# A recommender top on one core: one-hot products moved a period ahead, and a reordered head

## The chip, the cores and the metric

The kernel runs on one core of a Trainium2 chip. The metric is the device time of one execution in microseconds (us), as the median of several runs; lower is better.

## What is computed

The reference looks up 26 embedding rows for each of 2048 samples, forms all pairwise products of the 27 feature vectors of a sample (26 rows and a dense vector, 128 numbers each), and sends the result through three layers:

```python
e = jnp.stack([tbl_0[ids[:, 0]], ..., tbl_25[ids[:, 25]]], axis=1)     # (2048, 26, 128)
combined = jnp.concatenate([dense_output[:, None, :], e], axis=1)      # (2048, 27, 128)
interactions = jnp.einsum('bfd,bgd->bfg', combined, combined)
z = jnp.concatenate([dense_output, interactions[:, iu, ju]], axis=1)   # upper triangle, 351 pairs
h = jnp.concatenate([z, r_dense_output], axis=1)
h = jnp.maximum(h @ W_top1 + b_top1, 0.0)                              # 607 -> 512
h = jnp.maximum(h @ W_top2 + b_top2, 0.0)                              # 512 -> 256
y = h @ W_top3                                                         # 256 -> 1
```

All is float32. Eight of the tables have 1000 rows; the others have 1000 to 125000.

## The kernel before

**Tiling.** A duo is 256 samples (8 duos), a super is two duos (4 supers). A group is a pair of gathered tables for one duo: 18 tables are gathered, so a duo has 9 groups (T_GROUPS), 72 in all. The other 8 tables, of 1000 rows each, lie in SBUF as 125 partitions of 8 rows, each split in a rounded part (tab_hi) and a remainder (tab_lo), and are looked up by products with one-hot matrices.

**The steps**, as the code names them:
- "T": a group. POOL has gathered it in four indirect DMAs (line 239) into one of 5 slots of E; PE turns it (line 307, four transposes) into a PSUM bank; ACT copies it into ET (line 486).
- "hot": a chunk of one-hot products. DVE builds the one-hot of a chunk (line 552, ring of 3, so three chunks ahead of PE), PE multiplies (line 322, 8 matmuls: 4 blocks of rows, tab_hi and tab_lo). A duo has 16 chunks. Four chunks fill one bank, which ACT empties into ET (line 501). DVE needs the indices of four chunks from one transfer into oidx, a ring of 3 (line 247).
- "gram": 8 products of four samples' features with themselves (line 347) into one of two psG buffers; ACT copies one quarter (line 508), DVE places three more (line 574). A duo has 8 such fills. They read the ET half of their duo; ET has two halves, by d % 2.
- "C", "K": per super, the gram columns are turned (line 358) and copied to U (line 433), then turned as pairs (line 372), rounded (ACT, line 512) and split (DVE, line 583).
- "part": parts 0 to 3 are the first layer (lines 386 and 391, emptied at 460 and 462), 4 and 5 the second (line 398), 6 the third (line 405).

**What sets the order.** `steps_of(d)` writes out by hand the steps of period d, and PE, ACT, DVE and SP each go through the same list and do their share of each step, in order. Period d holds the turns of duo d, the grams of duo d - 1, chunks 8 to 15 of duo d between the grams, and chunks 0 to 7 of duo d + 1 after them; period 0 holds the first 24 chunks (all of duo 0, half of duo 1). Even periods add columns, pairs and parts 0 and 1 of a super, odd ones its parts 2 to 6. Period 8, the tail, has the last duo's grams and the last super's layers. `place_fills` gives the fills of T, hot, C, K and part one of three banks each, in step order. POOL only goes through the groups: it waits for the turn of group n - 5 before it gathers group n.

**The head.** SP issues the first part of the gather indices, then index transfers, the tables, the second part of the gather indices, the dense inputs, then the weights, and after these, going through the steps, the further index transfers from the fourth on (chunks 12 to 15 of duo 0), each once the one-hot that frees its place in the ring is built. The raw tables come into ET's second half, in six places (RAW), so tables 6 and 7 wait for the split of tables 0 and 1. ACT first makes tab_hi of all eight tables (`round_table`, line 469), then starts on the steps. DVE builds three one-hots, splits two tables (line 557), and then splits one more at every second chunk of period 0.

Of the kernel before, what the change touches and what calls it, by code (L numbers as in the profile page):

```python
# [13 lines left out]
def dlrm_program(nc, dense_pairs, dense_rows, gather_idx, hot_idx, gathered, small, W1_dense, W1_pairs,  # L14
# [20 lines left out]
    ROWS_P = ROWS // ROWS_K  # L35
    CHUNK_K = 4
    CHUNKS = NS * ROWS_K // CHUNK_K
    HALF_CHUNKS = CHUNKS // 2
    FILL_CHUNKS = 2 * ROWS_K // CHUNK_K
    RING = 3  # L40
    ID_RING = 3
    RAW = 6
    BANKS = 3

# [4 lines left out]
    KP = 3  # L49
# [9 lines left out]

    def steps_of(d):  # L60
        turns = [("T", d * T_GROUPS + i) for i in range(T_GROUPS)] if d < DUOS else []
        late = [("hot", d, c) for c in range(HALF_CHUNKS, CHUNKS)] if d < DUOS else []
        early = [("hot", d + 1, c) for c in range(HALF_CHUNKS)] if d + 1 < DUOS else []
        grams = [("gram", d - 1, i) for i in range(G_FILLS)]
        if d == 0:
            hot = [("hot", 0, c) for c in range(CHUNKS)] + early
            steps = hot[:4]
            for i, turn in enumerate(turns):
                steps += [turn] + hot[4 + 2 * i:6 + 2 * i]
            return steps + hot[4 + 2 * T_GROUPS:]  # L70
        if d == TAIL:
            u = SUPERS - 1
            return (grams + [("C", u, b) for b in range(C_BANKS)] + [("K", u, k) for k in range(KP)] +
                    [("part", u, p) for p in range(PARTS)])
        steps = []
        for i in range(G_FILLS):
            steps += [grams[i], late[i]]
            if i % 2 == 1:
                steps.append(turns[i // 2])
        rest = turns[G_FILLS // 2:]  # L80
        if d >= 2 and d % 2 == 0:
            u = d // 2 - 1
            columns = [("C", u, b) for b in range(C_BANKS)]
            pairs = [("K", u, k) for k in range(KP)]
            for i in range(HALF_CHUNKS):
                steps += early[i:i + 1] + columns[i:i + 1]
                if i % 2 == 1:
                    steps.append(rest[i // 2])
            steps += [pairs[0], pairs[1], rest[4], pairs[2]]
            return steps + [("part", u, 0), ("part", u, 1)]  # L90
        parts = [("part", d // 2 - 1, p) for p in range(2, PARTS)] if d >= 3 else []
        for i in range(HALF_CHUNKS):
            steps += early[i:i + 1]
            if i % 2 == 1:
                steps += [rest[i // 2]] + parts[i // 2:i // 2 + 1]
        return steps + [rest[4]] + parts[4:]

    PERIODS = range(TAIL + 1)
    STEPS = [step for d in PERIODS for step in steps_of(d)]
# [30 lines left out]
    with ctx:  # L130
# [114 lines left out]
        def _(sp):  # L245
# [5 lines left out]
                sp.dma_start(dense[:, d % 2], dense_pairs[d]).then_inc(dense_in[d % 2], 16)  # L251

            def load_table(h):
                sp.dma_start(raw_table(h), small[h].rearrange("(p k) d -> p (k d)", k=ROWS_K)  # L254
                             ).then_inc(table_in[h], 16)

            first = T_GROUPS * 4
            sp.dma_start(gidx[:, 0:first], gather_idx[:, 0:first]).then_inc(gidx_in[0], 16)
            load_oidx(0)
            load_table(0)  # L260
            load_table(1)
            sp.dma_start(gidx[:, first:], gather_idx[:, first:]).then_inc(gidx_in[1], 16)
            for h in range(2, RAW):
                load_table(h)
                if h == 3:
                    load_oidx(1)
                    load_oidx(2)
            load_dense(0)
            load_dense(1)
            for h in range(RAW, NS):  # L270
                sp.wait_ge(lo_ready, h - RAW + 1)
                load_table(h)
            sp.dma_start(raw_w1d, W1_dense.rearrange("a p n -> p a n")).then_inc(w1d_in, 16)
            sp.dma_start(raw_w1p, W1_pairs.rearrange("(k p) n -> p k n", k=KP)).then_inc(w1p_in, 16)
            sp.dma_start(w2[:, :, :], W2.rearrange("(k p) n -> p k n", p=P)).then_inc(weights_in, 16)
# [189 lines left out]
        @block.scalar  # L465
        def _(act):
            def round_table(h):
                act.wait_ge(table_in[h], 16)
                nc.scalar.copy(tab_hi[0:ROWS_P, h].rearrange("p k d -> p (k d)"),  # L469
                               raw_table(h)).then_inc(hi_ready, 1)  # L470

# [41 lines left out]

            act.wait_ge(ident_ready, 1)
            nc.scalar.copy(ident_r[:, :], ident[:, :]).then_inc(ident_r_ready, 1)
            for h in range(NS):
                round_table(h)
            for d in PERIODS:
                if d == 1:
                    round_W1()  # L520
# [4 lines left out]
                for step in steps_of(d):  # L525
                    if step[0] == "T":
                        empty_gathered(step[1])
                    elif step[0] == "hot" and step[2] % FILL_CHUNKS == FILL_CHUNKS - 1:
                        empty_hot(step[1], step[2])
                    elif step[0] == "gram":  # L530
                        empty_gram_first(step[1], step[2])
                    elif step[0] == "C" and on_scalar(step[1], step[2]):
                        empty_columns(nc.scalar, step[1], step[2])
                    elif step[0] == "K":
                        round_pairs(step[1], step[2])
                    elif step[0] == "part" and step[2] % 2 == 0:
                        empty_part(nc.scalar, step[1], step[2])
# [144 lines left out]
```

## Time and profile before

| | us |
|---|---|
| median of 3 runs (431.76 to 432.88) | 431.84 |
| the profiled execution | 434.48 |
| its span, first to last instruction | 432.7 |
| PE busy (matmuls) | 369.9 (86%) |
| POOL busy | 276.1 (64%) |
| DVE busy | 256.5 (59%) |
| ACT busy | 114.2 (26%) |
| mean granted TensorE clock | 0.942 |

The profile was taken of one execution, which was 2.6 us over the median; 1.8 us of it lie outside the span. Issuing of DMAs isn't counted as busy, so POOL's share is only the part of a gather that its engine records. Matmuls overlap, and a busy PE isn't PE at its peak. A clock of 1.00 is 2.4 GHz, one of 0.50 is 1.2 GHz.

### The profile page before, as it was taken

The numbers are of one execution on the slowest core, as the hardware profiler recorded it, in microseconds if no ns is written. First come the engines' busy times: TensorE is split into PE (matmuls) and PEld (weight loads), VectorE is DVE, ScalarE is ACT, GpSimd is POOL, SyncE is SP. The second block draws the span as 40 slices with busy tenths as digits, with TensorE's granted clock in tenths as the row PEclk, the third lists the DMA queues.
The fourth block names the chain that finished last, engine by engine and source line by source line (L and its number), as shares of the span: only waits on it lengthen the run. The fifth ranks groups of instructions, "written<-read, shape, count | busy, mean of one in ns | idle before, by whom it ended". The sixth has DMA issues, their size and how long they took to land.

```text
span 432.7 us, 6765 instructions
## 1 busy us (share of the span) xinstructions
PE 369.9 (86%) x2792; PEld 332.1 (77%) x2792; DVE 256.5 (59%) x368; ACT 114.2 (26%) x235; POOL 276.1 (64%) x295
## 2 busy tenths in 40 slices
PE   0560499996499959999999999999999999999797
PEld 0450499996499948997799979986999799678663
DVE  3254199998088833875389838952588566106410
ACT  2110333322122331322232333322123412321210
POOL 6772277777777777777777777777777777710000
PEclk9996599999599969999999999999899999989999
DMA  5659535444244433444343424343433332310000
GB/s 129 178 165 231 183 84 117 87 79 101 52 93 79 98 56 54 87 100 106 55 91 79 103 52 92 78 100 79 93 77 77 56 53 53 78 21 0 2 0 1
DMA packets 50941, 35.89 MB, mean 83 GB/s; under 512 B 6136, under 2 KB 44664, under 8 KB 50912
## 3 DMA queue, kind: packets, MB, share of 16 engines
q0 software_dynamic: 41472, 18.89, 24.7%
q1 hardware_dynamic: 9440, 16.58, 13.0%
q8 instruction: 22, 0.36, 0.3%
q14 instruction: 7, 0.06, 0.0%
HBM read 35.44 MB, written 0.01 MB: 82 GB/s over the span
## 4 chain that ended last, share of the span: by engine, by line
PE 58%; POOL 18%; issue 7%; DMA 6%; SPq 5%; DVE 3%; ACT 2%; DVEq 0%
POOL E L239 18%; PE psG L347 17%; PE psB L322 16%; PE psB L391 8%; PE psB L398 6%; DMA ET<-tbl 6%; PE psB L386 4%; PE psB L307 3%; SPq L254 2%; PE psB L358 2%; PE psB L405 2%; SPq L251 1%; SPq L247 1%; DVE S L574 1%; PE psB L372 1%
## 5 line engine op out<-in xcount | busy, mean ns | idle before, releaser
L239 POOL DMA_INDIRECT E<-tbl,gidx x288 | 275.4, 956 | 103.9 <-issue 87.0
L552 DVE TENSOR_TENSOR one_hot<-oidx,psR 125x1024 fp32r<-125x1024 int32 x128 | 152.3, 1215 | 39.0 <-PE psB L322 32.2
L322 PE MATMUL psB<-one_hot,tab_hi 125*128 125x256 f32 x512 | 143.2, 311 | 19.5 <-DVE tab_lo L557 13.4
L322 PE MATMUL psB<-one_hot,tab_lo 125*128 125x256 f32 x512 | 133.4, 292 | 0.0
L322 PEld LDWEIGHTS psB<-one_hot,tab_hi 125*128 125x128 f32 x512 | 103.0, 201 | 21.7 <-issue 13.8
L347 PE MATMUL psG<-ET 128*108 128x108 f32 x1024 | 112.5, 265 | 2.0 <-ACT ET L486 1.0
L347 PEld LDWEIGHTS psG<-ET 128*108 128x108 f32 x1024 | 106.6, 180 | 3.1 <-DVE S L574 1.6
L574 DVE COPY_PREDICATED S<-own,psG 108x216 f32<-108x216 int32 x192 | 77.1, 402 | 51.1 <-ACT S L508 44.5
L322 PEld LDWEIGHTS psB<-one_hot,tab_lo 125*128 125x128 f32 x512 | 103.1, 201 | 0.6 <-issue 0.5
L307 PE MATMUL psB<-ident_r,E 128*128 128x128 f32 x288 | 36.7, 253 | 32.0 <-ACT ET L501 18.3
L307 PEld LDWEIGHTS psB<-ident_r,E 128*128 128x128 f32 x288 | 31.0, 145 | 36.4 <-issue 20.0
L486 ACT COPY ET<-psB 128x512 f32<-128x512 f32 x72 | 42.3, 589 | 62.1 <-PE psB L307 62.0
L508 ACT COPY S<-psG 108x216 f32<-108x216 f32 x64 | 21.7, 340 | 110.1 <-PE psG L347 109.3
L398 PE MATMUL psB<-UH,w 128*128 128x512 f32 x64 | 29.0, 599 | 0.0
L462 DVE TENSOR_SCALAR UH<-psB,b1s 128x512 f32<-128x512 f32 x8 | 6.0, 751 | 36.6 <-PE psB L391 36.6
L501 ACT COPY ET<-psB 128x512 f32<-128x512 f32 x32 | 18.8, 586 | 30.9 <-PE psB L322 30.9
L391 PE MATMUL psB<-Zp_hi,w1p_hi 128*128 128x512 f32 x48 | 26.2, 545 | 0.0
L398 PEld LDWEIGHTS psB<-UH,w 128*128 128x128 f32 x64 | 11.7, 189 | 12.1 <-issue 12.0
L391 PE MATMUL psB<-Zp_hi,w1p_lo 128*128 128x512 f32 x48 | 19.3, 402 | 0.0
L391 PE MATMUL psB<-Zp_lo,w1p_hi 128*128 128x512 f32 x48 | 19.3, 401 | 0.0
L469 ACT CAST tab_hi<-ET 125x1024 fp32r<-125x1024 f32 x8 | 8.4, 1045 | 38.4 <-DMA ET<-tbl 38.4
L386 PE MATMUL psB<-Zd,w1d 128*128 128x512 f32 x32 | 18.0, 645 | 0.6 <-DVE Zp_lo L583 0.5
(34 smaller groups left out, 149.7 us busy)
## 6 DMA issues: line engine op xcount, KB each, us to landing
oidx<-hot_idx SPq DMA_DIRECT2D x32, 256.0 KB, 3.5
E<-tbl,gidx POOLq DMA_INDIRECT x288
ET<-tbl SPq DMA_DIRECT2D x8, 500.0 KB
dense<-dense_pairs SPq DMA_DIRECT2D x8, 128.0 KB, 3.6
Zd<-dense_rows SPq DMA_DIRECT2D x4, 256.0 KB, 3.1
UH<-W_pairs SPq DMA_DIRECT2D x1, 768.0 KB, 18.6
S<-W_dense SPq DMA_DIRECT2D x1, 512.0 KB, 21.1
w<-W SPq DMA_DIRECT2D x1, 512.0 KB, 13.4
```

Source lines behind the costliest of these rows:

```text
L239: nc.gpsimd.indirect_dma_start(E[:, n % SLOTS, i, :], None, gathered[2 * (n % T_GROUPS) + i // 2].bitcast(f32r), bass.IndirectOffsetOnAxis ...
L307: turned = nc.tensor.transpose(bank[:, i * P:(i + 1) * P].bitcast(f32r), E[:, n % SLOTS, i, :], ident_r[:, :])
L322: product = nc.tensor.matmul(bank[:, t % 2 * DUO:(t % 2 + 1) * DUO], tab[0:ROWS_P, t, r, :], one_hot[0:ROWS_P, m % RING, kc, :], start=(r ...
L347: gram = nc.tensor.matmul(psG[g % 2][0:M, a // 4, a % 4 * M:(a % 4 + 1) * M], four, four, start=True, stop=True)
L386: nc.tensor.matmul(bank[:, :], w1d[:, cols], Zd[:, :], start=True, stop=False)
L391: layer = nc.tensor.matmul(bank[:, :], w[:, kp, cols], z[:, kp, :], start=False, stop=(kp == KP - 1 and w is w1p_lo))
L398: layer = nc.tensor.matmul(bank[:, :], w2[:, q, cols], h1[:, q, :], start=(q == 0), stop=(q == M1 - 1))
L486: nc.scalar.copy(features(d, 1 + 2 * pair, 2), bank[:, :].rearrange("p (f j s) -> p f j s", f=2, s=GROUP)).then_inc(emptied, 1)
L501: nc.scalar.copy(features(d, f, 2), psB[bank][:, :].rearrange("p (f j s) -> p f j s", f=2, s=GROUP)).then_inc(bank_out[bank], 1)
L508: nc.scalar.copy(gram_rows(d, i), gram_samples(g, 0)).then_inc(G_first[g % 2], 1)
L552: nc.vector.tensor_tensor(one_hot[0:ROWS_P, m % RING], ids, rows, ALU.is_equal).then_inc(hot_full[m % RING], 1)
L574: copied = nc.vector.copy_predicated(gram_rows(d, i), mine, gram_samples(g, q))
```

## The change

- Chunks: `steps_of` puts all 16 chunks of duo d + 1 in period d, behind the 8 gram fills of duo d - 1. Period 0 has all 32 chunks of duos 0 and 1 (five, then three behind each turn), period 7 none.
- Between the grams stand the turns 0 to 3 of the duo and, in odd periods, parts 2 and 3; between the chunks stand turns 4 to 8, and columns and pairs or parts 4 to 6. Parts 0 and 1 stay at the end of even periods. In period 7 the last turn comes behind part 6.
- ACT rounds two tables before the steps and the other six at chunks 0, 2, 4, 6, 8 and 10 of duo 0.
- Each table comes in two transfers, of 112 and of 13 partitions, and ACT waits for both.
- SP: the second index transfer and the first dense load come behind three tables; the third index transfer behind six; the second part of the gather indices and the second dense load behind all tables.

```diff
+    SPREAD_P = ROWS_P // 16 * 16
...
-        late = [("hot", d, c) for c in range(HALF_CHUNKS, CHUNKS)] if d < DUOS else []
-        early = [("hot", d + 1, c) for c in range(HALF_CHUNKS)] if d + 1 < DUOS else []
+        hots = [("hot", d + 1, c) for c in range(CHUNKS)] if d + 1 < DUOS else []
         grams = [("gram", d - 1, i) for i in range(G_FILLS)]
         if d == 0:
-            hot = [("hot", 0, c) for c in range(CHUNKS)] + early
-            steps = hot[:4]
+            hots = [("hot", 0, c) for c in range(CHUNKS)] + hots
+            steps = hots[:5]
             for i, turn in enumerate(turns):
-                steps += [turn] + hot[4 + 2 * i:6 + 2 * i]
-            return steps + hot[4 + 2 * T_GROUPS:]
+                steps += [turn] + hots[5 + 3 * i:8 + 3 * i]
+            return steps
...
+        among_grams = {i: [turns[i // 2]] for i in range(1, G_FILLS, 2)}
+        rest = turns[G_FILLS // 2:]
+        among_hots = {1 + 3 * i: [turn] for i, turn in enumerate(rest)}
+        if d % 2 == 0:
+            u = d // 2 - 1
+            for b in range(C_BANKS):
+                among_hots.setdefault(3 + b, []).append(("C", u, b))
+            for k in range(KP):
+                among_hots.setdefault(12 + k, []).append(("K", u, k))
+            late = [("part", u, 0), ("part", u, 1)]
+        else:
+            u, late = d // 2 - 1, []
+            if u >= 0:
+                for i, p in enumerate(range(2, M1)):
+                    among_grams.setdefault(2 + 3 * i, []).append(("part", u, p))
+                for i, p in enumerate(range(M1, PARTS)):
+                    among_hots.setdefault(3 + 4 * i, []).append(("part", u, p))
         steps = []
         for i in range(G_FILLS):
...
+            steps += [grams[i]] + among_grams.get(i, [])
+        for i in range(CHUNKS):
+            steps += hots[i:i + 1] + among_hots.get(i, [])
+        return steps + late
...
             def load_table(h):
-                sp.dma_start(raw_table(h), small[h].rearrange("(p k) d -> p (k d)", k=ROWS_K)
-                             ).then_inc(table_in[h], 16)
+                rows = small[h].rearrange("(p k) d -> p (k d)", k=ROWS_K)
+                for part in (slice(0, SPREAD_P), slice(SPREAD_P, ROWS_P)):
+                    sp.dma_start(raw_table(h)[part], rows[part]).then_inc(table_in[h], 16)
...
             load_oidx(0)
-            load_table(0)
-            load_table(1)
-            sp.dma_start(gidx[:, first:], gather_idx[:, first:]).then_inc(gidx_in[1], 16)
-            for h in range(2, RAW):
+            for h in range(RAW):
                 load_table(h)
-                if h == 3:
+                if h == 2:
                     load_oidx(1)
-                    load_oidx(2)
-            load_dense(0)
-            load_dense(1)
+                    load_dense(0)
+            load_oidx(2)
             for h in range(RAW, NS):
                 sp.wait_ge(lo_ready, h - RAW + 1)
                 load_table(h)
+            sp.dma_start(gidx[:, first:], gather_idx[:, first:]).then_inc(gidx_in[1], 16)
+            load_dense(1)
...
-                act.wait_ge(table_in[h], 16)
+                act.wait_ge(table_in[h], 32)
...
-            for h in range(NS):
+            for h in range(2):
                 round_table(h)
+            rounded_tables = 2
...
-                    elif step[0] == "hot" and step[2] % FILL_CHUNKS == FILL_CHUNKS - 1:
-                        empty_hot(step[1], step[2])
+                    elif step[0] == "hot":
+                        if d == 0 and step[2] % 2 == 0 and rounded_tables < NS:
+                            round_table(rounded_tables)
+                            rounded_tables += 1
+                        if step[2] % FILL_CHUNKS == FILL_CHUNKS - 1:
+                            empty_hot(step[1], step[2])
```

## Rows read from the trace of the kernel before

Timeline rows: start us, us, engine, line, operation, out<-in with shapes, count, and in brackets the engine's idle time before and what ended it.

**Rows 1.** Waits, whole span: who waited for whom, total us, times, longest us

```profile
POOL E L239 <- issue: 87.0, 285, 0.3
POOL E L239 <- PE psB L307: 14.9, 1, 14.9
```

**Rows 2.** Timeline of POOL: the first gather, three others, the last

```profile
3.27 1.09 POOL L239 DMA_INDIRECT E<-tbl,gidx  x1 [1.70 <-DMA gidx<-gather_idx]
...
30.55 0.94 POOL L239 DMA_INDIRECT E<-tbl,gidx  x1 [0.31 <-issue]
...
50.69 0.94 POOL L239 DMA_INDIRECT E<-tbl,gidx  x1 [14.93 <-PE psB L307]
...
111.28 0.94 POOL L239 DMA_INDIRECT E<-tbl,gidx  x1 [0.31 <-issue]
...
379.92 0.94 POOL L239 DMA_INDIRECT E<-tbl,gidx  x1 [0.30 <-issue]
```

**Rows 3.** Timeline of PE: turns that end a duo, and the tail's grams

```profile
113.78 0.75 PE L307 MATMUL psB<-ident_r,E 128*128 128x128 f32 x4 [4.40 <-DMA E<-tbl,gidx]
115.50 0.85 PE L347 MATMUL psG<-ET 128*108 128x108 f32 x3 [0.98 <-ACT ET L486]
...
382.61 0.82 PE L307 MATMUL psB<-ident_r,E 128*128 128x128 f32 x4
...
385.86 6.41 PE L347 MATMUL psG<-ET 128*108 128x108 f32 x48
...
392.46 3.29 PE L347 MATMUL psG<-ET 128*108 128x108 f32 x32 [0.20 <-DVE S L574]
```

**Rows 4.** Windows: length, busy PE PEld DVE ACT POOL, PEclk, DMA share, GB/s

```profile
32.00:50.00 18.00, 0.31 (x3) 0.34 (x3) 4.71 (x4) 4.51 (x7) 3.15 (x3) 0.57 0.78 212
...
109.70:120.00 10.30, 5.24 (x27) 5.09 (x28) 0.79 (x2) 1.22 (x3) 7.55 (x10) 0.50 0.29 51
...
154.00:164.00 10.00, 7.04 (x25) 5.12 (x25) 2.08 (x3) 2.93 (x5) 7.56 (x9) 0.50 0.31 55
...
168.00:214.00 46.00, 45.36 (x347) 39.65 (x346) 30.10 (x43) 11.63 (x24) 34.71 (x38) 1.00 0.40 85
214.00:256.80 42.80, 42.09 (x354) 39.46 (x354) 31.11 (x46) 14.02 (x32) 32.12 (x36) 1.00 0.39 81
...
347.30:385.90 38.60, 37.92 (x284) 31.91 (x282) 17.43 (x32) 10.34 (x22) 25.34 (x27) 1.00 0.30 55
385.90:432.70 46.80, 40.28 (x243) 31.51 (x243) 15.00 (x33) 8.01 (x21) 0.00 (x0) 0.94 0.00 1
```

**Rows 5.** Timeline of ACT: first and last table cast, and the first emptying

```profile
9.61 1.04 ACT L469 CAST tab_hi<-ET 125x1024 fp32r<-125x1024 f32 x1 [7.28 <-DMA ET<-tbl]
...
48.02 1.04 ACT L469 CAST tab_hi<-ET 125x1024 fp32r<-125x1024 f32 x1 [2.84 <-DMA ET<-tbl]
48.97 0.58 ACT L501 COPY ET<-psB 128x512 f32<-128x512 f32 x1
```

**Rows 6.** DMA issues, 0 to 60 us: count, KB each, median us to landing

```profile
oidx<-hot_idx SPq DMA_DIRECT2D x6, 256.0 KB, 6.8
...
dense<-dense_pairs SPq DMA_DIRECT2D x2, 128.0 KB, 18.8
```

**Rows 7.** Timeline of SP's queue: two of its longest rows

```profile
33.22 7.24 SPq L275 DMA_DIRECT2D w<-W  x1
...
47.31 10.52 SPq L247 DMA_DIRECT2D oidx<-hot_idx  x3
```

**Rows 8.** Timeline of DVE: one-hots built without a wait

```profile
59.66 15.91 DVE L552 TENSOR_TENSOR one_hot<-oidx,psR 125x1024 fp32r<-125x1024 int32 x14
```

**Rows 9.** Chain that ended last, in order: start us, us, what

```profile
168.14 1.52 PE psG L347 x16
169.65 0.97 PE psB L322 x8
...
173.42 1.57 PE psG L347 x16
```

More of the change, by code:

```diff
@@ L37, in dlrm_program @@
     CHUNKS = NS * ROWS_K // CHUNK_K
-    HALF_CHUNKS = CHUNKS // 2
     FILL_CHUNKS = 2 * ROWS_K // CHUNK_K
@@ L74, in steps_of @@
                     [("part", u, p) for p in range(PARTS)])
+        among_grams = {i: [turns[i // 2]] for i in range(1, G_FILLS, 2)}
[15 more added lines that the diff above has]
+                    among_hots.setdefault(3 + 4 * i, []).append(("part", u, p))
         steps = []
         for i in range(G_FILLS):
[L77 to L96, printed above, removed]
+            steps += [grams[i]] + among_grams.get(i, [])
+        for i in range(CHUNKS):
+            steps += hots[i:i + 1] + among_hots.get(i, [])
+        return steps + late
     PERIODS = range(TAIL + 1)
```

## The prediction

> **What bounds the kernel now.** I first asked for the waits of the whole span [rows 1]. POOL, which issues the 288 gathers of line 239, is held up by another engine exactly once, for 14.9 us; its other gaps are 0.3 us of its own issue. The POOL timeline [rows 2] shows the place: the 24th gather ends at 35.76 us (50.69 less 14.93), the next starts at 50.69. Outside that hole one gather takes 0.94 + 0.30 = 1.24 us, so a duo's 36 gathers take 44.8 us, and the last one (379.92 + 0.94) ends at 380.86. Nothing else delays POOL, so the last gather can only come earlier if the hole closes or the long gathers at the head shorten.
>
> Is the last gather what the end waits for? The turn of the last group starts at 382.61 [rows 3], 1.75 us after that gather; the turn of the 18th group, for which PE did wait (4.40 us, on the gather), started 1.56 us after its gather (111.28 + 0.94 = 112.22). So PE arrives at the last turn within about 0.2 us of its data: both queues end together. After it come part 6 of the perceptron (3.25 us from the turn's start to the first gram), then 46.8 us of tail with POOL empty [rows 4].
>
> The windows [rows 4] give PE's load by period: 46.0 us for period 3 (odd: five perceptron parts), 42.8 for period 4 (even: columns, pairs, two parts), 38.6 for period 7. The mean of an odd and an even one, 44.4, is 0.4 under POOL's 44.8. A head change that speeds up POOL alone would therefore gain almost nothing, because PE would be late next; that is why the second half of the change matters.
>
> Why the hole: ACT rounds all 8 tables before it empties any bank. The casts start between 9.61 and 48.02 us, 5.5 us apart on average, and the first emptying is at 48.97 [rows 5]. PE has three banks, fills them, and stops; POOL has five slots, fills them and one more, and stops.
>
> **The change, step by step.**
>
> 1. ACT rounds two tables ahead, the other six at every second one-hot chunk. Same eight casts, no new work. The turns then need banks emptied early, which ACT now does. Gain up to 14.9 us on POOL. New waiting order: behind each cast stand the emptyings, so a late table still holds the banks.
>
> 2. Tables in 112 + 13 partitions. Before, one table of 500 KB lands each 5.5 us (93 GB/s), though in 32 to 50 us the queues together moved 212 GB/s at a share of 0.78 [rows 4, 5]. Dense loads of 128 KB took 18.8 us to land [rows 6]: behind the tables something is far fuller than the mean share says. The price is 8 more issues on SP. An issue that isn't blocked takes 0.3 to 0.6 us; the two rows at [rows 7] that last 7 and 10 us are blocked or waiting ones. Eight at 0.5 are 4 us of SP, beside transfers that take longer.
> The Trainium skill (DMA: Bandwidth & Descriptors, "Why a DMA increments its semaphore by 16 and not by 1") says that such a copy is spread over the largest number up to 16 that divides its outer size: 5 engines for 125 rows, 16 for 112, 13 for 13. The slow landing of the tables at a middling share agrees. By the rule the tables would cease to be the limit; the sum doesn't use it beyond the bounds in step 3.
>
> 3. Period 0 now holds 32 chunks instead of 24, and three chunks instead of two between turns. So the turn of group 3 needs the one-hot of chunk 13, and that needs the fourth index transfer (chunks 12 to 15). This transfer stands on SP behind everything of the head: the tables, the second part of gidx, both dense loads, W1, W2, biases, Zd. That is the new dependency. Before, it was issued at 47.31 and with 6.8 us landed at 54.1 [rows 6, 7]; nobody minded, as the turns had come to a halt for other reasons. Bytes up to and including it: tables 4000, four index transfers 1024, W1 1280, W2 512, Zd 256, dense 256, gidx 144 KB, in all 7.65 MB. Gathers take 65.6 KB per 1.24 us = 53 GB/s beside it. At 212 GB/s in all, 159 are left: 48 us, landing at 49.5. At 212 / 0.78 = 272, 219 are left: 35 us, landing at 36.5. I take 36, since 272 is what the engines gave while they were busy and that is what an even spread should reach.
> After the landing DVE owes three operations of 1.14 us (chunk 12, the eighth split, chunk 13; pace from 14 builds in 15.91 us [rows 8]), then PE one chunk, at most 1.94 us (twice the 0.97 of [rows 9]), and a turn: some 6 us, so the turn of group 3 is done at 42. When is it needed? Group 5's gathers start at 30.55 [rows 2], group 8's three groups of 4.98 later, at 45.5, and they need the slot of group 3. So 3.5 us to spare: no stall. Later turns follow three chunks apart, 3.4 us by DVE's pace when PE is at 2.4 GHz, against POOL's 4.98.
> **Sum of steps 1 to 3: -14.9 us on POOL** (at worst, from landing at 49.5: a new hole of 49.5 + 6 - 45.5 = 10 us).
>
> 4. All one-hot products one period early. The work is the same (128 chunks of 0.97 us, 64 gram fills of 1.52 [rows 9]); eight chunks, 7.8 us, move from period 7 to period 0. Period 0 then ends at about 61 us, bound by DVE: after the landing at 36 it has some 22 operations of 1.14 left. Period 1 is 8 fills, 16 chunks at DVE's 1.14 and 9 turns of 0.30 (168.14 to 173.42, less two fills and two chunks [rows 9]), 33 us, so 94. POOL's last group for it, without the hole, lands at 98.9 (the turn that waited for it started at 113.78 [rows 3], less 14.9). So PE has caught up with POOL by the end of period 1, with eight chunks more done than before. From there an even period must end 9.3 us after POOL's last group (two chunks, pair 2, parts 0 and 1 come after the last turn), an odd one somewhat later, and the sum of both is 88.8 against 89.6: PE stays level. In period 7 PE needs 38.6 - 7.8 = 30.8; it starts 9.3 behind, so it is ready for the last turn after about 40 of POOL's 44.8 us. **Four to five us of slack, on the path nothing.** The gain of the move is that step 1's 14.9 us aren't swallowed by PE.
>
> 5. Grams without chunks between them. In the tail, where they already run so, two fills take 3.29 us and a wait of 0.20 for DVE's placing [rows 3]. In a period two fills and a turn are 2 x 1.52 + 0.30 = 3.34. Loss 0.15 x 4 = 0.6 us a period; in odd periods parts 2 and 3 lie between and cover it. I take +0.5 in all, after slack; if it were 0.6 in each of periods 3 to 7 and clock losses came on top, it reaches +4.
>
> 6. End of period 7: part 6 now comes before the last turn. From the last turn's start to the first gram it was 3.25 us; where nothing stood between, at period 2's start, it was 1.72 (113.78 to 115.50) [rows 3]. **-1.5 us.**
>
> 7. Clock. PE now waits about 3 us before the last turn. After such waits the granted clock was 0.50 for 10.3 us (109.7 to 120 [rows 4]), that is 1.2 GHz. In the tail of before only the first gram fills were slow: three in the first 6.6 us, where the warm pace gives 3.49 for two. A longer slow stretch costs 0 to 2.5 more; **+1.5.**
>
> Total: -14.9 + 0 + 0.5 - 1.5 + 1.5 = -14.4 us. Profiled: span 432.7 to 418.3, its time 434.48 to 420.1. The median of the runs, 431.84, is 2.6 below the profiled execution; the same sum makes it **417.4**.
>
> **Rivals.**
> A. The head's fourth index transfer is late. For it: SP is in order, and 7.65 MB stand before it. Against it: the transfers of before were slow at a low mean share. Landing at 49.5 makes a hole of 10 us: 427. If the split brought nothing at all and it landed at 54.1 as before, 14.6 us: 432, no change. This is also the case that the change doesn't do what it says.
> B. PE becomes the bound in periods 3 to 7: its slack of 4 to 5 us is eaten by one clock stretch (10.3 us at half pace costs up to 5.1) and by the gram blocks (3): 4 us past the slack, 421.
> C. Slower: the clock. With eight chunks out of the way PE waits for gathers in each of periods 2 to 7, where in the trace it waits for none after period 2. Place: those waits; price: 5.1 us for a stretch like that of 109.7; it decides from the fourth stretch on (4 x 5.1 less the slack of 4.5 is 15.9, more than the gain of 14.4). With six, 30.6 - 4.5 = 26 us: 443.5. Against it: a slow PE falls behind, then doesn't wait, and recovers; before shows two stretches (109.7 and 154 [rows 4]) and none of that length later.
> The Trainium skill (TensorE: Matmul & The Clock Gate, "HAM oscillation — how this bites in real kernels") tells of kernels in which each wait for data throttles the engine anew, which speaks against this change; by it C would be the outcome. The trace has the effect twice, and shows it ending when PE falls behind.
>
> **Chances.** Forecast (415 to 420) 0.62; A with a partial hole (420 to 430) 0.12; B (419 to 424) 0.17; A in full, about 432, 0.04; C 0.05. Range: step by step the low end is 414 (no clock loss, slightly shorter issue of the head's gathers: the six groups before the hole end at 35.76, where 3.27 + 24 x 1.24 would be 33.0), the high end 425, which leaves out C, the full A and half of the partial one. About 1.3 us, 0.3%, can be told from no change: faster 0.91, same 0.04, slower 0.05.
>
> **What would show it.** The POOL timeline without a gap over 0.4 us: steps 1 to 3 right; a gap at the group after 45 us, with DVE waiting for oidx before it: A. Tables landing 2 to 3 us apart: step 2. PE waiting 2 to 5 us for the last gather in period 7: step 4; no wait there and parts back to back: B. The first gram 1.7 us after the last turn's start: step 6. Granted clock under 0.9 in periods 3 to 7: C. The prediction is wrong if the last gather ends elsewhere than at 366, or if the stretch from it to the end isn't 52 us.

## The result, and the profile after

| | before | changed |
|---|---|---|
| median, us | 432.36 (431.76 to 433.13, 4 runs) | 420.91 (419.24 to 422.60, 4 runs) |
| profiled execution, us | 434.48 | 419.24 |
| its span, us | 432.7 | 417.0 |
| mean granted clock | 0.942 | 0.965 |

The ratio is 0.9734, with a 95% interval of 0.9691 to 0.9778. The kernel is faster by 11.4 us in the medians and by 15.7 us in the two profiled spans: the profiled execution of the kernel before lies above all four of its runs, that of the changed kernel is the fastest of its four. What follows explains the 15.7 us of the two traces, some 4 us more than the medians differ by. The forecast was 417.4, in a range of 414 to 425. Medians are of all executions of a kernel in its job; where too few of them lay within 1.5% of its fastest, no ratio is given.

The POOL timeline of the changed kernel (start us, us, engine, line, operation; in brackets the idle time before) stands against [rows 2]. Line 239 is now line 240.

```profile
28.47 1.85 POOL L240 DMA_INDIRECT E<-tbl,gidx  x1 [0.30 <-issue]
...
39.34 1.89 POOL L240 DMA_INDIRECT E<-tbl,gidx  x1 [0.31 <-issue]
...
47.75 0.94 POOL L240 DMA_INDIRECT E<-tbl,gidx  x1 [0.30 <-issue]
...
365.86 0.94 POOL L240 DMA_INDIRECT E<-tbl,gidx  x1 [0.31 <-issue]
```

The hole is gone. The last gather ends at 366.80 instead of 380.86: 14.1 us, against a hole of 14.9. The missing 0.8 to 0.9 us are small things: the gathers are busy 275.9 us instead of 275.4 (two of 1.85 and 1.89 us in the head are shown), and their gaps without the hole are 89.3 instead of 89.0, with a start of the first gather that is 0.07 later.

ACT's timeline, against [rows 5]: the casts of the tables, now 1.2 to 4.8 us apart (2.9 on average) instead of 5.5, with emptyings between them.

```profile
8.20 1.04 ACT L469 CAST tab_hi<-ET 125x1024 fp32r<-125x1024 f32 x1 [5.87 <-DMA ET<-tbl]
10.38 1.04 ACT L469 CAST tab_hi<-ET 125x1024 fp32r<-125x1024 f32 x1 [1.14 <-DMA ET<-tbl]
12.88 1.04 ACT L469 CAST tab_hi<-ET 125x1024 fp32r<-125x1024 f32 x1 [1.46 <-DMA ET<-tbl]
...
20.62 0.58 ACT L486 COPY ET<-psB 128x512 f32<-128x512 f32 x1
...
28.32 1.05 ACT L469 CAST tab_hi<-ET 125x1024 fp32r<-125x1024 f32 x1 [0.17 <-DMA ET<-tbl]
```

DVE's timeline shows the new dependency of step 3, the fourth index transfer:

```profile
29.43 1.21 DVE L557 TENSOR_TENSOR one_hot<-oidx,psR 125x1024 fp32r<-125x1024 int32 x1
38.05 1.22 DVE L557 TENSOR_TENSOR one_hot<-oidx,psR 125x1024 fp32r<-125x1024 int32 x1 [7.42 <-DMA oidx<-hot_idx]
39.19 1.22 DVE L562 TENSOR_TENSOR tab_lo<-ET,tab_hi 125x1024 fp32r<-125x1024 f32 x1
```

Last, PE at the end of period 7, against [rows 3]: the last turns (line 307), parts 5 and 6 (lines 398 and 405), the first gram of the tail.

```profile
358.40 0.53 PE L307 MATMUL psB<-ident_r,E 128*128 128x128 f32 x4 [1.75 <-DMA E<-tbl,gidx]
358.77 3.67 PE L398 MATMUL psB<-UH,w 128*128 128x512 f32 x8
363.44 0.53 PE L307 MATMUL psB<-ident_r,E 128*128 128x128 f32 x4 [1.01 <-DMA E<-tbl,gidx]
363.81 1.91 PE L405 MATMUL psB<-w3s,h 128*128 128x1 f32 x16
368.41 0.75 PE L307 MATMUL psB<-ident_r,E 128*128 128x128 f32 x4 [2.69 <-DMA E<-tbl,gidx]
369.99 4.19 PE L347 MATMUL psG<-ET 128*108 128x108 f32 x23 [0.83 <-issue]
```

So the 15.7 us of the spans come as follows: last gather 14.1 earlier; its turn 1.6 us behind it instead of 1.75 (0.1); first gram 1.58 us after the turn's start instead of 3.25 (1.7); tail 47.0 us instead of 46.8 (-0.2).

### The profile page after: what moved, and what is told of

The parts are those of the page before. It is cut to its first block, busy times and chain, and to the rows that moved or that the text cites. A ratio compares the mean times of both kernels' runs of the same rounds, so it can differ in the third digit from the quotient of the medians.

```text
span 417.0 us, 6773 instructions
## 1 busy us (share of the span) xinstructions
PE 365.8 (88%) x2792; PEld 328.6 (79%) x2792; DVE 257.2 (62%) x368; ACT 114.4 (27%) x235; POOL 276.7 (66%) x295
## 3 DMA queue, kind: packets, MB, share of 16 engines
q1 hardware_dynamic: 9632, 16.58, 14.9%
## 4 chain that ended last, share of the span: by engine, by line
POOL 53%; PE 23%; issue 18%; DMA 3%; DVE 2%; ACT 1%; POOLq 0%
POOL E L240 53%; PE psG L347 7%; PE psB L391 5%; PE psB L322 4%; DMA E<-tbl,gidx 2%; PE psB L386 2%; PE psB L398 2%; PE psB L358 2%; PE psB L307 1%; DVE S L579 1%; PE psB L372 1%; DVE one_hot L557 1%; PE psB L405 0%; DMA gidx<-gather_idx 0%; DVE Zp_lo L588 0%
## 5 line engine op out<-in xcount | busy, mean ns | idle before, releaser
L240 POOL DMA_INDIRECT E<-tbl,gidx x288 | 275.9, 958 | 89.3 <-issue 87.0
L557 DVE TENSOR_TENSOR one_hot<-oidx,psR 125x1024 fp32r<-125x1024 int32 x128 | 149.3, 1214 | 35.5 <-PE psB L322 23.4
L322 PE MATMUL psB<-one_hot,tab_hi 125*128 125x256 f32 x512 | 139.1, 307 | 21.4 <-DVE tab_lo L562 11.1
L322 PE MATMUL psB<-one_hot,tab_lo 125*128 125x256 f32 x512 | 131.0, 290 | 0.0
L347 PE MATMUL psG<-ET 128*108 128x108 f32 x1024 | 108.8, 265 | 3.5 <-DVE S L579 2.3
L347 PEld LDWEIGHTS psG<-ET 128*108 128x108 f32 x1024 | 104.7, 180 | 6.1 <-DVE S L579 3.3
L307 PEld LDWEIGHTS psB<-ident_r,E 128*128 128x128 f32 x288 | 29.9, 143 | 24.3 <-DMA E<-tbl,gidx 23.6
L391 PE MATMUL psB<-Zp_hi,w1p_hi 128*128 128x512 f32 x48 | 25.2, 526 | 0.0
L358 PE MATMUL psB<-ident,S 108*128 108x108 f32 x104 | 16.3, 287 | 1.8 <-issue 1.8
L386 PE MATMUL psB<-Zd,w1d 128*128 128x512 f32 x32 | 16.7, 603 | 0.5 <-DVE Zp_lo L588 0.5
```

Of the source, the lines that this page charges most:

```text
L240: nc.gpsimd.indirect_dma_start(E[:, n % SLOTS, i, :], None, gathered[2 * (n % T_GROUPS) + i // 2].bitcast(f32r), bass.IndirectOffsetOnAxis ...
L307: turned = nc.tensor.transpose(bank[:, i * P:(i + 1) * P].bitcast(f32r), E[:, n % SLOTS, i, :], ident_r[:, :])
L322: product = nc.tensor.matmul(bank[:, t % 2 * DUO:(t % 2 + 1) * DUO], tab[0:ROWS_P, t, r, :], one_hot[0:ROWS_P, m % RING, kc, :], start=(r ...
L347: gram = nc.tensor.matmul(psG[g % 2][0:M, a // 4, a % 4 * M:(a % 4 + 1) * M], four, four, start=True, stop=True)
L358: turned = nc.tensor.transpose(bank[:, i * M:(i + 1) * M], S[0:M, :, c], ident[0:M, 0:M])
L386: nc.tensor.matmul(bank[:, :], w1d[:, cols], Zd[:, :], start=True, stop=False)
```

## The experiments

**Which part of the change closes the hole?** Four kernels, run on one chip together with the kernel before (434.28, 431.74 to 438.04, 19 runs). The kernel before took 1.9 us longer here than in the job of the result (432.36), and the changed kernel wasn't in this job; the expectations were worked out from the figures of that one.

*head_only*: the new head with the old steps (an extract, against the changed kernel).

```diff
     def steps_of(d):
...
+        late = [("hot", d, c) for c in range(HALF_CHUNKS, CHUNKS)] if d < DUOS else []
+        early = [("hot", d + 1, c) for c in range(HALF_CHUNKS)] if d + 1 < DUOS else []
```

> The head of the changed kernel (split table transfers, SP's order, ACT rounding between chunks) with the steps of the kernel before. Theory 1, the prediction's step 4: PE, level with POOL before, is late next and swallows the 14.9 us; last gather near 366 but last turn 8 to 14 us behind its data, 428 to 431 us. Theory 2: PE stood still in the same hole, so both queues move together; last turn within 1 us of its data, part 6 still behind it, 418 to 420 us.

Measured: 421.79 us (419.05 to 423.42), ratio 0.9666 (0.9586 to 0.9746). The time is 1.8 us above theory 2's 418 to 420, in a job in which the kernel before took 1.9 us longer, and well under theory 1's 428 to 431: theory 1 falls. PE at the end of its period 7:

```profile
366.89 0.86 PE L307 MATMUL psB<-ident_r,E 128*128 128x128 f32 x4
...
370.69 0.86 PE L307 MATMUL psB<-ident_r,E 128*128 128x128 f32 x4
372.19 1.92 PE L405 MATMUL psB<-w3s,h 128*128 128x1 f32 x16 [0.64 <-ACT ET L486]
373.97 6.40 PE L347 MATMUL psG<-ET 128*108 128x108 f32 x48
```

Its last gather ends at 366.14 (the group's turn waits for it no longer), so with the 1.6 us of the changed kernel its data are there at 367.7 and the turn comes 3 us late, not within 1 us as theory 2 had it, and not 8 to 14. With part 6 behind it the first gram is at 373.97, 4.0 us later than in the changed kernel's trace: 2.3 because the turn is later (370.69 against 368.41), 1.7 for part 6's place (3.28 us from turn to gram against 1.58), which is step 6 and not the chunks. The best executions of both kernels are level (419.05 and 419.24), and the intervals overlap. So the move of the chunks is worth between nothing and the 2.3 us of these two traces, not the whole gain.

*move_only*: the new steps with the old head, each table in one transfer again (an extract).

```diff
             def load_table(h):
-                rows = small[h].rearrange("(p k) d -> p (k d)", k=ROWS_K)
-                for part in (slice(0, SPREAD_P), slice(SPREAD_P, ROWS_P)):
-                    sp.dma_start(raw_table(h)[part], rows[part]).then_inc(table_in[h], 16)
+                sp.dma_start(raw_table(h), small[h].rearrange("(p k) d -> p (k d)", k=ROWS_K)
+                             ).then_inc(table_in[h], 16)
...
             first = T_GROUPS * 4
             sp.dma_start(gidx[:, 0:first], gather_idx[:, 0:first]).then_inc(gidx_in[0], 16)
             load_oidx(0)
+            load_table(0)
+            load_table(1)
...
-            for h in range(2):
+            for h in range(NS):
                 round_table(h)
```

> The steps of the changed kernel with the head of the kernel before. Theory 1 (POOL is the bound, its hole stays near 14.9 us): last gather at 381 as before, gain only from the last turn's order, 429.5 to 432 us. Theory 2 (PE was the bound from period 3 on): the 7.8 us taken out of period 7 show, 423 to 426 us.

Measured: 432.92 us (432.49 to 435.74, 10 runs), ratio 0.9953 (0.9917 to 0.9989). Theory 1 in the mechanism: 0.9 us above its 429.5 to 432, and far from theory 2's 423 to 426. POOL's hole is where it was:

```profile
34.73 0.94 POOL L240 DMA_INDIRECT E<-tbl,gidx  x1 [0.31 <-issue]
50.67 0.94 POOL L240 DMA_INDIRECT E<-tbl,gidx  x1 [15.00 <-PE psB L308]
```

The 0.5% that is left, some 2 us, is of the size of step 6 (the last turn's order). PE at the end of this trace:

```profile
382.20 0.53 PE L308 MATMUL psB<-ident_r,E 128*128 128x128 f32 x4 [1.50 <-DMA E<-tbl,gidx]
383.56 7.61 PE L348 MATMUL psG<-ET 128*108 128x108 f32 x48 [0.83 <-issue]
```

The first gram is 2.3 us earlier than before (383.56 against 385.86), 1.9 of it between turn and gram (1.36 against 3.25). But this execution's tail took 50.3 us instead of 46.8; that comes up again under step 7.

*act_first*: the changed kernel, ACT rounding all tables first.

```diff
-            for h in range(2):
+            for h in range(NS):
                 round_table(h)
-            rounded_tables = 2
+            rounded_tables = NS
```

> The changed kernel, but ACT rounds all eight tables before it empties a bank, as before. Theory 1 (the split alone closes the hole): last table lands near 27.6, ACT is free near 29, turn of group 1 before the 35.5 at which POOL needs its slot; no hole, within 1 us of the changed kernel, 420 to 422 us. Theory 2 (ACT's order closes it): a hole of 8 us or more, 428 us or more.

Measured: 421.42 us (419.08 to 422.58), ratio 0.9657 (0.9586 to 0.9729). Theory 1: the interleaving on ACT is worth nothing once the tables come fast, and POOL waits for PE nowhere in this trace. ACT's last cast and first emptyings:

```profile
26.96 1.05 ACT L469 CAST tab_hi<-ET 125x1024 fp32r<-125x1024 f32 x1 [1.25 <-DMA ET<-tbl]
27.91 0.58 ACT L501 COPY ET<-psB 128x512 f32<-128x512 f32 x1
28.39 0.41 ACT L492 COPY ET<-dense 128x256 f32<-128x256 f32 x1
28.69 0.59 ACT L486 COPY ET<-psB 128x512 f32<-128x512 f32 x1
```

The first emptying is at 27.91 instead of 48.97; the kernel before ran out of slots at 35.76.

*no_spread*: the changed kernel, each table in one transfer.

```diff
-                rows = small[h].rearrange("(p k) d -> p (k d)", k=ROWS_K)
-                for part in (slice(0, SPREAD_P), slice(SPREAD_P, ROWS_P)):
-                    sp.dma_start(raw_table(h)[part], rows[part]).then_inc(table_in[h], 16)
+                sp.dma_start(raw_table(h), small[h].rearrange("(p k) d -> p (k d)", k=ROWS_K)
+                             ).then_inc(table_in[h], 16)
```

> The changed kernel, but each table in one transfer of 125 partitions. Theory 1, rival A of the prediction: the fourth index transfer lands near 54 behind slow tables, the turn of group 3 ends near 60, POOL has a hole of 12 to 15 us in the ninth group, 430 to 434 us. Theory 2 (ACT's interleaving alone suffices): no hole, 420 to 423 us.

Measured: 434.93 us (433.91 to 436.19, 10 runs), ratio 1.0014 (0.9978 to 1.0050): the whole gain is gone. Theory 1 (0.9 us above its 430 to 434), rival A of the prediction. Its POOL and DVE timelines, where three holes have come in place of one:

```profile
36.55 0.94 POOL L240 DMA_INDIRECT E<-tbl,gidx  x1 [1.95 <-PE psB L306]
...
44.73 0.94 POOL L240 DMA_INDIRECT E<-tbl,gidx  x1 [3.52 <-PE psB L306]
...
62.42 0.94 POOL L240 DMA_INDIRECT E<-tbl,gidx  x1 [13.03 <-PE psB L306]
```

```profile
44.71 1.21 DVE L556 TENSOR_TENSOR one_hot<-oidx,psR 125x1024 fp32r<-125x1024 int32 x1
56.52 1.22 DVE L556 TENSOR_TENSOR one_hot<-oidx,psR 125x1024 fp32r<-125x1024 int32 x1 [10.59 <-DMA oidx<-hot_idx]
```

DVE gets the indices at 56.5, PE's turn of group 3 starts at 61.69, and POOL, which needs that slot, goes on at 62.42. The long hole is the ninth group's, as rival A has it.

So of the head's parts the split of the transfers carries the gain: without it all is lost, without ACT's new order nothing is. SP's new order wasn't tried by itself, and neither was the kernel before with nothing but the split.

**What binds now?** The remaining kernels ran in later hours, when the kernel before itself took 527 to 530 us; their times can be compared with it and with each other in the same job, not with those above, and the changed kernel wasn't in these jobs. None of their expectations, which are in us of the usual hours, can be judged by the times; what they still tell stands in the traces.

*part6_last*: part 6 behind the last turn of period 7, as before.

```diff
+        if d == DUOS - 1:
+            steps.remove(("part", u, PARTS - 1))
+            late = [("part", u, PARTS - 1)]
         return steps + late
```

> The changed kernel with part 6 behind the last turn of period 7, as before. Theory 1 (step 6 of the prediction): from the last turn's start to the first gram 3.2 to 3.3 us instead of 1.6, so 1.6 us slower than the changed kernel, about 422.5 us. Theory 2: PE's longer idle time ahead of the last turn cools the clock as well, 423 to 425 us.

Measured: 515.58 us (501.63 to 520.1) beside 527.3 for the kernel before. In this trace the last two turns stand together:

```profile
466.69 1.53 PE L310 MATMUL psB<-ident_r,E 128*128 128x128 f32 x8
468.19 1.92 PE L408 MATMUL psB<-w3s,h 128*128 128x1 f32 x16
469.97 5.26 PE L350 MATMUL psG<-ET 128*108 128x108 f32 x36
```

The last four of the eight transposes start at 467.68, 1.6 us behind the last gather (466.08), so the first gram comes 2.3 us after the last turn's start: 0.7 more than the changed kernel's 1.6, and less than the 3.25 of before, where PE also waited 0.65 us for ACT ahead of part 6. Inconclusive by itself; the usual hours tell more: 3.25 us (before) and 3.28 (head_only) with part 6 behind the turn, 1.36 (move_only) and 1.58 (the changed kernel, act_first, no_spread) without.

*chunks_back*: chunks 8 to 15 of the last duo back between the grams of period 7.

```diff
+        if d == DUOS - 2:
+            hots = hots[:CHUNKS // 2]
+        back = [("hot", d, c) for c in range(CHUNKS // 2, CHUNKS)] if d == DUOS - 1 else []
         for i in range(G_FILLS):
-            steps += [grams[i]] + among_grams.get(i, [])
+            steps += [grams[i]] + back[i:i + 1] + among_grams.get(i, [])
```

> The changed kernel, but chunks 8 to 15 of the last duo go back into period 7, between its grams. Theory 1 (step 4's slack): PE waited 1.75 + 1.01 + 2.69 = 5.5 us for gathers in period 7; 7.8 us more work make the last turn 2.3 us later, and PE has no idle time that cools the clock; 421 to 424 us. Theory 2 (the slack has no worth): same as the changed kernel within 1 us, the clock giving back what the work takes. Theory 3 (the move carries the gain): 427 us or more.

Measured: 516.14 us (512.95 to 517.98), ratio to the kernel before of that job 0.9774 (0.9694 to 0.9854). It keeps a gain of the relative size of the changed kernel's (0.9734). Theory 3's 427 us would be 0.988 of 432.36, or 0.983 of 434.28, which the interval includes, and a gain in per cent need not carry over to these hours. So it speaks against theory 3 only weakly; head_only is the evidence against it. Theories 1 and 2 aren't told apart.

*fewer_gathers* and its repeats: the fourth gather of each group of duos 3 and 4 is left out, so the outputs lack the rows that it would have brought.

```diff
-                for i in range(4):
+                for i in range(3 if n in FEWER else 4):
                     nc.gpsimd.indirect_dma_start(
```

> The changed kernel without the fourth gather of each group of duos 3 and 4 (18 gathers, 22.4 us of POOL, left out; the turn takes what lies in the slot). Theory 1 (POOL alone is the bound): 22 us faster, 399 us. Theory 2 (PE is level with POOL from period 2 on, with the 5.5 us of waits in period 7 and a few in periods 4 and 6 as all its slack): 5 to 9 us faster, 412 to 416 us, and PE waits for no gather in period 7.

> The changed kernel without the fourth gather of each group of duos 3 and 4 (18 gathers, 22.4 us of POOL left out, the turn takes what lies in the slot), on another chip. Theory 1 (POOL alone is the bound): 22 us faster, 399 us. Theory 2 (PE is level with POOL; its 5.5 us of waits in period 7 and some in periods 4 and 6 are all its slack): 5 to 9 us faster, 412 to 416 us, no wait of PE for a gather in period 7.

> The changed kernel without the fourth gather of each group of duos 3 and 4 (18 gathers, 22.4 us of POOL left out, the turn takes what lies in the slot), taken again in the same hour. Theory 1 (POOL alone is the bound): 22 us faster, 399 us. Theory 2 (PE is level with POOL; its 5.5 us of waits in period 7 and some in periods 4 and 6 are all its slack): 5 to 9 us faster, 412 to 416 us, no wait of PE for a gather in period 7.

Measured: 498.78, 494.95 and 495.02 us beside 527.3, 530.12 and 526.55; ratios 0.9473 (0.9403 to 0.9542) in the first and 0.9381 (0.9304 to 0.9458) in the third. Beside chunks_back in the first job it is 17.4 us faster. The turns of these traces show where: from the last turn of duo 2 to that of duo 4 it is 118.0 us in chunks_back (190.10 to 308.09) and 97.7 in fewer_gathers (184.32 to 282.06). In all traces of these hours it is 113.6 to 119.7 with all gathers (five traces) and 97.0 to 98.4 without (three). The other duos scatter: duo 5 takes 60.1 in both of the first job, duo 6 48.3 in chunks_back and 56.7 in fewer_gathers. So 15 to 23 us are saved just where gathers are missing, of their 22.4, although POOL waited for PE for 58 to 70 us in these traces (0.6 us in the changed kernel's trace), 38 us of it around these two duos (190 to 310 us of fewer_gathers). The first theory's size comes out under conditions in which it should not, and the second's test, the slack in a usual hour, wasn't had. Inconclusive for the question it was made for.

*half_first* and its repeats: the last duo is gathered in another order, all 18 tables of its first 128 samples and then those of the second, so that four of its gram fills can run in period 7 in PE's waits.

```diff
+        if d == DUOS - 1:
+            for i, turn in enumerate(turns[5:]):
+                at = steps.index(turn) + 1 + (i == 2)
+                steps.insert(at - (i == 2), ("gram", d, i))
...
+    def source(n, i):
+        if n // T_GROUPS < DUOS - 1:
+            return i % 2, 2 * (n % T_GROUPS) + i // 2
+        return divmod(4 * (n % T_GROUPS) + i, NG)
```

> The changed kernel, with the last duo gathered in another order: all 18 tables of its first 128 samples, then those of the second; its first four gram fills then run in period 7, in the gaps where PE waits for gathers. Theory 1: the tail loses four fills of 1.75 us, period 7 gains at most 1 us, and PE stays warm into the tail; 6 to 8 us faster than the changed kernel, 413 to 415 us. Theory 2: PE's 5.5 us of waits don't hold four fills of 1.52 us and their evictions, the last turn comes late by 3 us or more: 416 to 419 us.

> The changed kernel with the last duo gathered half by half of its samples, and four of its gram fills in period 7, as in half_first, on another chip. Theory 1: four fills of 1.75 us leave the tail, 6 to 8 us faster than the changed kernel's 420.9, 413 to 415 us. Theory 2: the four fills don't fit in PE's waits of period 7, the last turn comes 3 us or more late: 416 to 419 us.

> The changed kernel with the last duo gathered half by half of its samples, and four of its gram fills in period 7, taken again in an hour in which the kernel before should run near its usual 432 to 434 us. Theory 1: four fills of 1.75 us leave the tail; 6 to 8 us faster than the changed kernel's 420.9, so 413 to 415 us. Theory 2: the four fills don't fit in PE's waits of period 7, the last turn comes 3 us or more late: 416 to 419 us.

Measured: 513.67, 504.36 and 510.89 us beside 527.3, 530.12 and 526.55; ratios 0.9528 (0.9468 to 0.9587) in the second and 0.9739 (0.9674 to 0.9804) in the third. PE around the last turn (line 318; grams are line 361) in the third:

```profile
450.55 1.73 PE L361 MATMUL psG<-ET 128*108 128x108 f32 x16
452.06 0.52 PE L318 MATMUL psB<-ident_r,E 128*128 128x128 f32 x4
452.41 1.73 PE L361 MATMUL psG<-ET 128*108 128x108 f32 x16
...
457.73 1.73 PE L361 MATMUL psG<-ET 128*108 128x108 f32 x16
...
461.02 0.51 PE L318 MATMUL psB<-ident_r,E 128*128 128x128 f32 x4
461.37 3.25 PE L361 MATMUL psG<-ET 128*108 128x108 f32 x32
```

From the last turn's start to the end of the span it is 40.6 us here (501.6 - 461.02), 40.5 in the first run and 42.9 in the second, against 48.6 in the changed kernel (417.0 - 368.41) and 48.3 to 50.4 in chunks_back and the three fewer_gathers, in the hours of these runs: the stretch behind the last turn is 5.4 to 9.9 us shorter, as theory 1 has it. But the last turn starts 7.3, 11.1 and 7.3 us behind the last gather in the three runs, where it is 1.6 to 6.3 in the other traces of these hours, so theory 2's late turn may be in it too. Whether the end comes earlier when PE isn't late anyway, and so whether this kernel beats the changed one, stays open: it was never timed against it under the usual conditions.

## Why the prediction was right

The time is in the range and the mechanism of the head is the one that was forecast, but the number needed some luck. 420.91 lies just above the 415 to 420 that was called the forecast and given 0.62, and inside B's and A's brackets, though neither happened: POOL has no hole, and PE waited for the last gather. One step, the fourth, was wrong in its conclusion. By terms of the two traces:

| us | forecast | traces |
|---|---|---|
| steps 1 to 3, last gather | -14.9 | -14.1 |
| step 4, last turn behind its gather | 0 | -0.1 |
| step 5, gram blocks | +0.5 | 0 |
| step 6, turn to first gram | -1.5 | -1.7 |
| step 7, tail | +1.5 | +0.2 |
| sum | -14.4 | -15.7 |

By its own signs the prediction was to be wrong if the last gather ended elsewhere than at 366 or the stretch from it to the end wasn't 52 us. They are 366.80 and 50.2: the first is 0.8 off, the second 2, for steps 5 and 7, and the two errors partly cancel.

- **Steps 1 to 3, the hole.** Forecast 14.9 us, no new hole; measured 14.1, no new hole. The load of the head was the point that decided. The fourth index transfer was put at 36; DVE got it at 38.05. Group 3's turn was put at 42, ended at 44.1 (start 43.47), and POOL needed it at 47.75. The rate that was taken, 272 GB/s from the busy share of 32 to 50 us, was about right: the changed kernel moved 251 over its first 36 us. Most of the transfer's parts were there in time for the 36.5 (11 of 16 by 36.13), the last at 38.03. The other bound, 212, would have made a hole, and no_spread, where the head's transfers stay slow, has it: 13.0 us, and a kernel no faster than before. Rival A was priced at 432 for that case; 434.9 was measured. It was right that the split decides; it was wrong that ACT's order has a share (step 1's "up to 14.9"): act_first shows none.
- **Step 2, the split.** Over 4 to 24 us the changed kernel moved 253 GB/s, the one with single transfers 173.

```profile
4.00:24.00 20.00, 10.19 (x61) 9.31 (x61) 15.24 (x14) 7.55 (x9) 15.42 (x16) 1.00 1.14 253
```

```profile
4.00:24.00 20.00, 6.78 (x28) 6.22 (x29) 9.32 (x8) 3.13 (x3) 15.42 (x16) 1.00 0.63 173
```

  (Windows of the changed kernel and of no_spread: length, busy time of PE, PEld, DVE, ACT, POOL, granted clock, DMA share, GB/s.)

  The traces also keep the time of each landing that a semaphore counts, and these show the cause itself. Before, the first table has one count at 2.13 us, at its issue, and five when its data land (9.17 to 9.58); split, it has one and 29, and all have landed at 8.18. The tables are complete 2.2 to 4.1 us apart instead of 5.5. And the transfers issued behind single tables came in two parts: of the 16 landings of the first dense load, 11 came at 23.48 to 23.97 and the last five at 37.14 to 37.64; of the fourth index transfer, 11 by 50.23 and five at 53.59 to 54.09. In the changed kernel the first dense load's 16 came at 12.29 to 14.47. The rule of 5, 16 and 13 engines in the Trainium skill (DMA: Bandwidth & Descriptors, "Why a DMA increments its semaphore by 16 and not by 1") agrees with these counts, 5 and 16 + 13. A split into two parts that don't divide well (63 and 62, say) was not run.
- **Step 4, the move.** Its schedule came out as worked: PE waits for gathers at the ends of the even periods and in period 7, there 1.75, 1.01 and 2.69 us, 5.5 in all where 4 to 5 were forecast. But its conclusion failed, "the gain of the move is that step 1's 14.9 us aren't swallowed by PE", as did the sentence that a head change alone would gain almost nothing. The error is in the comparison: PE's rate per period equals POOL's, and from that I concluded that PE couldn't follow. But PE had stood still in the same hole (0.31 us busy from 32 to 50 us [rows 4]). When the hole closes, PE starts its even race earlier as well, and both ends move together: in head_only's trace the last gather ends 14.7 us earlier than before and the last turn starts 11.9 earlier, so PE swallowed 2.8 us and not 8 to 14. Its ratio (0.9666) is no worse than the changed kernel's. The total came out right because the step added nothing to the sum.
- **Step 5, gram blocks.** +0.5 was taken for a time that slack covers; PE is ready before the last data, so it cost nothing in this trace.
- **Step 6, the order of the last turn.** Forecast 1.72 us from turn to gram, -1.5; measured 1.58, -1.7.
- **Step 7, the clock.** Forecast +1.5 for a longer slow stretch. In the changed kernel's trace the granted clock was 0.50 from 367.0 to 373.7, nearly half of that stretch before the first gram at 369.99, and the tail took 47.0 us against 46.8: +0.2. That small price was luck of this execution. The other three traces of the usual hours in which PE also waited for the last gather have tails of 49.3 (act_first), 48.4 (no_spread) and 50.3 us (move_only), at mean granted clocks of 0.88, 0.92 and 0.84; head_only, in which it didn't wait, has 46.8 at 0.94, as before. So in these four traces it cost 0.2 to 3.5 us in the tail, and +1.5 was a fair price.

```profile
371.08:420.40 49.32, 42.79 (x242) 34.00 (x242) 15.00 (x33) 7.84 (x20) 0.00 (x0) 0.88 0.00 1
383.56:433.90 50.34, 44.60 (x242) 35.56 (x242) 15.17 (x33) 8.02 (x20) 0.00 (x0) 0.84 0.00 1
373.97:420.80 46.83, 40.32 (x244) 31.54 (x243) 14.97 (x33) 7.99 (x21) 0.00 (x0) 0.94 0.00 1
```

  (Tails of act_first, move_only and head_only.)
  Rival C, slow stretches in each period, didn't come: over 129 to 364 us the mean granted clock was 0.99, although PE waited for gathers there, at the ends of the even periods and in period 7, up to 1.75 us. The one slow stretch between 109 and 364 us (0.89 on average over 109 to 129) came with the longest wait for a gather of all, 3.80 us, which ended at 126.05. The Trainium skill's example (TensorE: Matmul & The Clock Gate, "HAM oscillation — how this bites in real kernels") has a wait of some 3 to 5 us in every round; the waits for gathers in periods 3 to 7 were shorter here. So this trace doesn't speak against the Trainium skill, and C failed because such waits didn't come in those periods.

```profile
129.00:364.00 235.00, 228.51 (x1775) 203.93 (x1774) 150.27 (x222) 67.84 (x147) 177.34 (x190) 0.99 0.38 77
367.00:373.70 6.70, 4.46 (x25) 4.30 (x26) 0.11 (x1) 0.93 (x2) 0.00 (x0) 0.50 0.07 12
```

- **From the span to the median.** The sum for the profiled execution, 420.1, was 0.9 above what was measured (419.24; in spans 418.3 against 417.0). The forecast median, 417.4, was 3.5 below the measured 420.91. The term that failed is the 2.6 us by which the profiled execution lay above the median of three runs. Those three lay at the low end: 19 later runs of the kernel before go from 431.74 to 438.04, with a median of 434.28, next to the profiled 434.48. That median less 14.4 is 419.9. Another part is that the changed kernel's profiled execution was its fastest; its other runs, of which no trace was kept, may have had longer tails like act_first's.

## What to carry to other kernels

When a queue has a hole, look whether the engine that seems to be the next bound stood still in the same hole: if so, closing it moves both, and equal rates are no reason to expect that the gain is swallowed. If transfers are slow at a middling share of the DMA engines, check how the outer size of the tile divides before reordering anything around them; here 112 + 13 partitions for 125 did what an engine's reordering couldn't. And a profiled execution is better taken at its own time; three runs don't tell where it lies among the others.

## What the hardware showed beyond that

In the later hours the kernel before took 22% longer (527 to 530 us), and the traces have something that those of a usual hour don't. By their semaphores the engines stood idle with all their waits fulfilled: in half_first_c 25 times on PE for more than 0.5 us, 40 us in all, 19 times on DVE (39 us) and 17 times on ACT (30 us), where the changed kernel's trace has two on PE (2.6 us in all) and none on DVE or ACT. Besides, the profile puts waits to an end by "remote", nothing that it shows: 26 of POOL's, 48 us in all, and none in the changed kernel's trace. But for one stop on PE (1.77 us, which the changed kernel's tail has too), all the stops lie before the end of the last gather; the stretch behind it had a granted clock of 1.00. The two windows of half_first_c:

```profile
0.00:453.70 453.70, 349.71 (x2548) 317.61 (x2548) 243.55 (x336) 103.69 (x213) 276.95 (x295) 0.89 0.37 79
453.70:501.60 47.90, 41.55 (x247) 30.99 (x245) 15.12 (x33) 9.32 (x23) 0.03 (x1) 1.00 0.01 2
```

The stops end with the gathers, and leaving gathers out of duos 3 and 4 saved 15 to 23 us in these duos although POOL waited for PE there. So they may go with the gathers' DMA traffic; that is a guess, for other work ends there too. What makes them wasn't found; no run was made for it, and this stays open.
